# A mixture-of-experts kernel: row gathers moved behind the puts, three blocks ahead, and the sums' base copied by ScalarE

## The reference

```
x = layernorm(x + attention(x))      # q, k softmax; ctx = k^T v; y = q ctx Wo + bo
x = layernorm(x + moe(x))

logits = x @ wr.T                    # 8 experts
vals, idx = top_k(logits, 2)         # two experts for each row
gating = softmax over the two
cap = 5120                           # rows that an expert takes at most
xg = rows of x by expert
h = gelu(xg @ w1[e] + b1[e])         # 256 -> 1024
y = h @ w2[e] + b2[e]                # 1024 -> 256
out[row] += gating * y               # segment_sum over rows
```

## Time and profile before

| | |
|---|---|
| median of 3 runs | 2240.74 us (2238.51 to 2243.51) |
| profiled execution | 2238.88 us |
| its span | 2237.1 us |
| TensorE busy | 2024.5 us, 90% |
| VectorE busy | 1523.5 us, 68% |
| ScalarE busy | 1129.9 us, 51% |
| GpSimd busy | 1248.0 us, 56% |
| mean granted clock of TensorE | 0.973 |
| chain that ended last, by engine | PE 38%, issue 14%, POOL 8%, DVE 7%, DMA 3% |

### The profile page before, as it was taken

The page is one execution under the profiler, slowest core; times in us unless marked ns, Lnnn a source line. Parts: engine busy times, 40 slices in busy tenths (PEclk is TensorE's granted clock), DMA queues, the critical chain, the costliest instruction groups (busy, mean ns, idle before and its releaser), DMA issues.

```text
span 2237.1 us, 53012 instructions
## 1 busy us (share of the span) xinstructions
PE 2024.5 (90%) x15708; PEld 1938.2 (87%) x15709; DVE 1523.5 (68%) x4485; ACT 1129.9 (51%) x2519; POOL 1248.0 (56%) x1323
## 2 busy tenths in 40 slices
PE   7999899998678998999998999999999999999996
PEld 6888888887668988998898999989989989998996
DVE  3776777777546677668667666776777676666675
ACT  3566566565443444545454455454545445454553
POOL 1366666666645555555555555555555555555554
PEclk9999999999778999999999999999999999999998
DMA  5243334332124434334433443354354444443443
GB/s 178 84 145 124 106 123 146 107 123 86 58 70 154 144 103 142 115 111 125 132 108 106 147 121 116 112 154 124 116 157 124 126 119 128 128 134 117 138 129 99
DMA packets 306950, 272.74 MB, mean 122 GB/s; under 512 B 167331, under 2 KB 276094, under 8 KB 305744
## 3 DMA queue, kind: packets, MB, share of 16 engines
q1 hardware_dynamic: 253264, 171.59, 25.8%
q0 software_dynamic: 45200, 84.85, 12.2%
q10 hardware_dynamic: 8432, 15.73, 2.1%
HBM read 186.58 MB, written 102.26 MB: 129 GB/s over the span
## 4 chain that ended last, share of the span: by engine, by line
PE 38%; issue 14%; POOL 8%; DVE 7%; DMA 3%; another core or an unknown queue 2%; ACT 2%; DVEq 1%; SPq 0%; POOLq 0%; ACTq 0%
PE y_ps L1768 22%; PE h_ps L1752 15%; POOL rows L1442 5%; DVE h_lo L1683 2%; POOL rstd_b L1448 2%; POOL out L1466 1%; DMA stage<-rows 1%; DVE y L1649 1%; DMA x<-stage 0%; DVE rstd_b L1642 0%; DVE rstd_b L1640 0%; DMA base<-stage 0%; DVE put_idx L1647 0%; DMA rows<-x_rows,pick_idx 0%
## 5 line engine op out<-in xcount | busy, mean ns | idle before, releaser
L1556 ACT ACTIVATE h_ps<-h_ps,b_sb 128x256 f32<-128x256 f32 x1000 | 404.8, 445 | 620.4 <-PE h_ps L1752 607.5
L1768 PE MATMUL y_ps<-w_hi,h_hi 128*128 128x256 f32 x2000 | 576.2, 288 | 103.3 <-DVE h_lo L1683 77.0
L1752 PE MATMUL h_ps<-bt_hi,w_hi 128*128 128x256 f32 x2000 | 557.3, 279 | 5.4 <-issue 3.3
L1768 PE MATMUL y_ps<-w_hi,h_lo 128*128 128x256 f32 x2000 | 560.7, 280 | 0.3 <-issue 0.3
L1768 PE MATMUL y_ps<-w_lo,h_hi 128*128 128x256 f32 x2000 | 560.5, 280 | 0.0
L1752 PE MATMUL h_ps<-bt_hi,w_lo 128*128 128x256 f32 x2000 | 555.8, 278 | 1.2 <-issue 1.2
L1752 PE MATMUL h_ps<-bt_lo,w_hi 128*128 128x256 f32 x2000 | 555.8, 278 | 0.0
L1768 PEld LDWEIGHTS y_ps<-w_hi,h_hi 128*128 128x128 f32 x2000 | 380.0, 190 | 130.7 <-DVE h_lo L1683 93.7
L1442 POOL DMA_INDIRECT rows<-x_rows,pick_idx x250 | 247.6, 990 | 367.8 <-issue 328.0
L1752 PEld LDWEIGHTS h_ps<-bt_hi,w_hi 128*128 128x128 f32 x2000 | 377.4, 189 | 8.3 <-issue 5.7
L1768 PEld LDWEIGHTS y_ps<-w_lo,h_hi 128*128 128x128 f32 x2000 | 379.9, 190 | 0.0
(11 more groups left out here) (281 smaller groups left out, 3453.2 us busy)
## 6 DMA issues: line engine op xcount, KB each, us to landing
stage<-rows SPq DMA_DIRECT2D x126, 256.0 KB, 2.2
x<-stage SPq DMA_DIRECT2D x504, 64.0 KB
base<-stage SPq DMA_DIRECT2D x125, 256.0 KB
xt_raw<-in_x_t SPq DMA_DIRECT2D x32, 512.0 KB
x_raw<-in_x SPq DMA_DIRECT2D x64, 256.0 KB
x_rows<-x_sb SPq DMA_DIRECT2D x32, 512.0 KB
out<-alone SPq DMA_DIRECT2D x32, 512.0 KB
w_raw<-in_w ACTq DMA_DIRECT2D x14, 1024.0 KB
```

The source lines that it names most:

```text
L1556: nc.scalar.activation(half, half, ACT.Gelu_apprx_tanh, bias=b1_sb[:, bass.ds(e * FT + 2 * g + i, 1)]).then_inc(gelu_done, 1)
L1752: ins = nc.tensor.matmul(h_ps[:, g, (f % 2) * BLK:(f % 2 + 1) * BLK], w[:, c:c + P], v[:, k, :], start=(i == 0), stop=(i == 3 * DK - 1))
L1768: ins = nc.tensor.matmul(y_ps[:, t, :], v[:, g, h:h + P], w[:, c:c + D], start=(f == 0 and t == 0 and part == 0), stop=(f == FT - 1 and t ...
```

## The change

GpSimd issues the gather for block n+3 at the end of its block n, behind the puts (in an expert's first block behind the puts too, and before the wait for their landing). The gather of the third block is issued once ahead of the loop. To have the indices, VectorE copies pick_idx for it between bt_lo and the gates, not at its block's head. The slot table gets one more block of padding. SyncE reads the next block's rows from staging into a new buffer x1_next a block early, and ScalarE copies them to base after the add, behind its first h_hi (in an expert's second block behind its third, since the add is later there). To say that by block, ScalarE's first two blocks of an expert are written out ahead of its loop. Two small unused tensors change size and place.

```diff
@@ sync
-                def load_base(n):
-
-                    sp.wait_ge(sum_step, STEPS * n + 1)
-                    sp.dma_start(base[:, :, :], block_of(n).rearrange("(t p) d -> p t d", p=P)).then_inc(base_done, 16)
+                def load_next(n):
+                    sp.dma_start(x1_next[:, :, :], block_of(n).rearrange("(t p) d -> p t d", p=P)).then_inc(next_loaded, 16)
...
+                load_next(0)
                 with sp.Fori(0, total) as n:
-                    load_base(n)
-                    sp.wait_ge(gathered, 16 * BT * (n + 2))
+                    wait_apart(sp, base_done, n + 1)
+                    load_next(n + 1)
+                    wait_apart(sp, gathered, 16 * BT * (n + 2))
                     store_rows(n + 2, rows, stored)
                     wait_apart(sp, xt_ready, n + 1)
                     load_x4(n + 2)
@@ gpsimd
                 def gather(n):
                     pool.wait_ge(stored, 16 * (n - 1))
-                    wait_apart(pool, pick_ready, n - 1)
+                    wait_apart(pool, pick_ready, n - 2)
...
                 def take_up_sums(n):
-                    pool.wait_ge(base_done, 16 * (n + 1))
+                    pool.wait_ge(base_done, n + 1)
...
                 def first_body(n, lays=()):
-                    gather(n + 2)
                     root(n)
                     put(n)
+                    gather(n + 3)
                     for e in lays:
                         lay_table(e)
                     pool.wait_ge(put_done, 16 * BT * (n + 1) + 16)
                     take_up_sums(n)
                 def body(n, lays=(None, None)):
-                    gather(n + 2)
                     root(n)
                     take_up_sums(n)
                     if lays[0] is not None:
                         lay_table(lays[0])
                     put(n, 1)
+                    gather(n + 3)
@@ scalar
+                def lay_base(n):
+                    act.wait_ge(sum_step, STEPS * n + 1)
+                    act.wait_ge(next_loaded, 16 * (n + 1))
+                    nc.scalar.activation(base[:, :, :], x1_next[:, :, :], ACT.Copy).then_inc(base_done, 1)
-                def body(n, e, eu, load=False):
+                def body(n, e, eu, late_base=0, load=False):
                     for g in range(UNITS):
...
+                        if g == late_base:
+                            lay_base(n)
...
-                    with act.Fori(0, 4) as block:
+                    body(before, e, eu)
+                    body(before + 1, e, eu, 2)
+                    with act.Fori(2, 4) as block:
                         body(before + block, e, eu)
@@ vector, body
-                    pick(n + 2)
...
                             split_lo(n + 1)
-                            if e == 0 and turn == 3:
-                                dve.wait_ge(table_padded, 4 + E - 1)
+                            if e == 0 and turn in (2, 3):
+                                dve.wait_ge(table_padded, 4 + (1 if turn == 2 else E - 1))
+                            pick(n + 3)
                             gates(n + 1)
```

More of the change, by code:

```diff
@@ L30, in build @@
     CLOSED = NB - 3
-    TCOLS = MINI * BT + E * CAP // P + 2 * BT
+    TCOLS = MINI * BT + E * CAP // P + 3 * BT
     SLOTS = TCOLS * P
@@ L87, in build @@
         mini_table = keep("mini_table", [P, MINI * BT, EW], I)
-        table_in = keep("table_in", [P, E * EC + 2 * BT, EW], I)
+        table_in = keep("table_in", [P, E * EC + 3 * BT, EW], I)
+        keep("aside", [P, 24])
         rows = keep("rows", [P, BT, D])
@@ L1329, in build @@
             TCOLS = E * EC
-            table = sb("table", [P, BT + TCOLS + 2 * BT, EW], I)
+            table = sb("table", [P, BT + TCOLS + 3 * BT, EW], I)
             pick_idx, base_idx, put_idx = (sb(f"{n}_idx", [P, BT], I) for n in ("pick", "base", "put"))
@@ L1336, in build @@
             rstd, mean, minus_half = sb("rstd_b", [P, BT]), sb("mean_b", [P, BT]), sb("minus_half_b", [P, BT])
-            sb("spare", [P, 32])
+            sb("spare", [P, 24])
             xt_hi, xt_lo = sb("bt_hi", [P, DK, BLK], R), sb("bt_lo", [P, DK, BLK], R)
@@ L1345, in build @@
             x4 = sb("x4", [P, BLK // 32, D // 4])
+            x1_next = sb("x1_next", [P, BT, D])
             h_ps = ps("h_ps", [P, UNITS, 2 * BLK])
@@ L1355, in build @@
             x4_loaded, first_turned = sem("x4_loaded"), sem("first_turned")
+            next_loaded = sem("next_loaded")
             base_done, base_loaded = sem("base_done"), sem("base_loaded")
@@ L1396, in load_x4 @@
                 def load_x4(n):
-                    sp.wait_ge(stored, 16 * n)
+                    wait_apart(sp, stored, 16 * n)
                     by_band = block_of(n).rearrange("(g j) (c e) -> c j g e", j=32, c=4)
@@ L1422, in _ @@
                     load_x4(n + 2)
-                sp.wait_ge(x4_loaded, 64 * (total + 1))
+                wait_apart(sp, x4_loaded, 64 * (total + 1))
+                wait_apart(sp, next_loaded, 16 * (total + 1))
                 wait_apart(sp, put_done, 16 * BT * (total + 1) + 16)
@@ L1494, in _ @@
                 pool.wait_ge(first_stored, 16)
+                wait_apart(pool, stored, 16)
+                wait_apart(pool, first_turned, 1)
+                for t in range(BT):
+                    pool.indirect_dma_start(
+                        out=rows[:, t, :], out_offset=None, in_=x1_dram,
+                        in_offset=bass.IndirectOffsetOnAxis(ap=table_in[:, 2 * BT + t, 0:1], axis=0)).then_inc(gathered, 16)
                 def first_body(n, lays=()):
-                    gather(n + 2)
                     root(n)
                     put(n)
+                    gather(n + 3)
                     for e in lays:
@@ L1537, in _ @@
                 put(total)
-                pool.wait_ge(gathered, 16 * BT * (total + 1))
+                pool.wait_ge(gathered, 16 * BT * (total + 2))
             @program.scalar
@@ L1569, in expert @@
                     blocks, before = blocks_of(act, e)
-                    with act.Fori(0, 4) as block:
+                    body(before, e, eu)
+                    body(before + 1, e, eu, 2)
+                    with act.Fori(2, 4) as block:
                         body(before + block, e, eu)
-                    body(before + 4, e, eu, load)
+                    body(before + 4, e, eu, 0, load)
                     with act.Fori(5, blocks) as block:
@@ L1594, in pick @@
                 def pick(n):
-                    dve.wait_ge(gathered, 16 * BT * (n - 1))
+                    wait_apart(dve, gathered, 16 * BT * (n - 1))
                     V.tensor_copy(pick_idx[:, :], column(n + 1, 0)).then_inc(pick_ready, 1)
```

3 lines of the change are left out of this document (1 added, 2 removed).

## The result

| | median of the runs, us | runs |
|---|---|---|
| before | 2239.62 (2233.19 to 2243.51) | 4 |
| after | 2330.59 (2323.49 to 2350.87) | 4 |

The ratio is 1.042, 95% interval 1.035 to 1.049: slower, where 2165 us and faster was forecast. The kernel before does not always take this long: in one of the five sets of runs that follow it took 2122 us, in the other four 2226 to 2238 us, so a kernel is compared only with the kernel before of its own set.

A forecast was written before the change was run, and what follows sets the result against it. TensorE was taken as the bound, losing time waiting before `down(1)` for VectorE's h_lo behind a late root. Terms -88 + 8 + 0 + 4 = -76 us took 2238.88 to 2163, median 2165; own range 2142 to 2195, overall 2142 to 2230.

The forecast's parts named there:

- R3: Rival, chance 0.09: indirect DMAs over every block's head release VectorE and ScalarE 1.9 us late; 2366 us.
- Root earlier in each block: GpSimd's root starts 0.80 us earlier, closing TensorE's gap before `down(1)` in 113 blocks: 88 us saved, 54 to 98.
- What is late next: After the gap closes, TensorE's own pace sets the block: steady blocks 11.1 to 11.2 us apart.
- over 11.5 was the sign of being wrong: Sign that the forecast is wrong: TensorE's period from block to block stays over 11.5 us.
- Some 1.7 us of slack: GpSimd's block: its six indirect DMAs end at 2101.7, 1.7 us before the next variance at 2103.4.
- ScalarE's copy waits for nothing: ScalarE's 624 ns base copy behind the first h_hi finds the add done; cost taken as 0.
- ScalarE's code: Longer written-out ScalarE code may bring one more long wait at each of three jumps: 4 us taken, 0 to 13.
- Second blocks of an expert: There VectorE's add waits for base sums that come later: 1.0 us, 8 times, 8 us given back; 0 to 15.
- R1: Rival, chance 0.15: another step of VectorE's chain holds the second h_lo, 0.4 us left in each of 113 blocks; 2210 us.
- R2: Rival, chance 0.09: the moved gathers on GpSimd hold VectorE's add, taking 0.6 of the 0.9 us; 2219 us.
- R4: Rival, chance 0.07: GpSimd's gathers stay late behind pick_idx or the store, root as late as before; 2241 to 2253 us.

The follow-up runs named there:

- set A: First of the five sets of follow-up runs, all its kernels on one chip; the kernel before took 2122.35 us.
- sp_rows: Changed kernel without GpSimd's row gathers, SyncE reading rows in order instead: 2034.51 us, ratio 0.959; rerun 2108.45 us, 0.943.
- gather_only: Changed kernel with only the moved gathers and late pick_idx copy, base read by SyncE as before: 2080.37 us, 0.981; rerun 2459.82 us, 1.103.
- base_only: Changed kernel with gathers and pick_idx copy where they were before, base still copied by ScalarE from the early read: 2129.83 us, ratio 1.003.
- gate_swap: Changed kernel with gathers at GpSimd's block head behind y_raw, VectorE's root wait behind the second pair's h_lo: 2165.06 us, 0.970; rerun 2163.69 us, 0.968.
- set C: Third set of follow-up runs, varying how many and which DMAs GpSimd issues; the kernel before took 2236.14 us.
- set E: Last set of follow-up runs, on the same chip as set A; kernel before 2237.78 us, changed kernel again 2331.97 us, ratio 1.043.

## Why the prediction was wrong

The step that failed is the argument against R3, "the put at 1454.70 stands over a block's head too, and the add followed its data", which left it 0.09. That put does not stand over a head. The head is at 1453.01, and its y_raw started at 1453.32, 1.4 us before the put: the signal was through. The next one was not. The head, y_raw and ScalarE's first gelu of that block, in the trace of before:

```profile
1453.01 0.28 PE L1752 MATMUL h_ps<-bt_hi,w_hi 128*128 128x256 f32 x1
...
1453.32 0.69 DVE L1708 TENSOR_TENSOR y_raw<-y_ps,b_sb 128x512 f32<-128x512 f32 x1
...
1456.64 0.81 ACT L1556 ACTIVATE h_ps<-h_ps,b_sb 128x256 f32<-128x256 f32 x2 [6.57 <-PE h_ps L1752]
```

The gelu stands 3.63 us after the head, where 1.7 is usual, and 0.95 us after the put's end at 1455.69. The very block that was read against the rival shows it, as the earlier trace rows do (885.70 is 0.93 us after the put's end). Counting would have told: in 19 of 124 blocks of that trace an indirect DMA is in progress at the head, and in 12 of them y_raw starts over 1 us or the gelu over 2.2 us after it; of the other 105 it is 4. The count also shows what stays unexplained: in four of the 19 it is a gather of sums (base), and y_raw was prompt in all four, 1453.01 among them.

So the shift did not bring its 88 us, and the loss stands elsewhere than R3 had it. R3's formula, 1.9 us late less 0.9 us earlier in each of 113 blocks, puts the loss before `down(1)`. That gap did not change; the 100.8 us of the loop stand before `down(0)` and in TensorE's own stops, which neither the forecast nor R3 had. That R3's 2366 us comes near 2331 is in part luck.

Term by term:

- Root earlier in each block, 88 us: right in mechanism. The root is prompt, and in set A, where nothing is held, sp_rows gained 87.8 us. That the two agree so well is luck: sp_rows leaves out the gathers altogether, and gather_only, which has them, gained 42.0 us.
- What is late next: y_raw. It is 1.83 us later in the steady block, of which the prompt root gives 0.57 back (0.9 was forecast). The median distance of two heads rose from 12.00 to 13.18 us; 11.1 to 11.2 was forecast, and over 11.5 was the sign of being wrong.
- "Some 1.7 us of slack" on GpSimd was right in kind: its last gather ends before the next variance. It was beside the point: the question was where its DMAs lie, not whether they are done.
- ScalarE's copy waits for nothing: wrong here, 38.8 us in 86 blocks, because y_raw and the gelu start together, and 9.1 us once in the first block. In set A copy, longer code and early read cost 7.5 us together, against 0 + 4.
- ScalarE's code, 4 us: the waits with no known releaser, from which this was priced, did not come with the longer code: base_only has it and not one such wait.
- Second blocks of an expert, 8 us: waits of the adds for gathered sums rose from 10.5 to 16.5 us.
- R1, R2, R4 did not come: the second h_lo waits for y_raw's chain, the add follows y_raw by 0.12 us in the block shown, the gathers are not late. The 52 adds that ran beside an indirect DMA took 486 ns on average, the others 482.

## What to carry to other kernels

Ask of a moved indirect DMA not only whether it fits into GpSimd's block, but which signals of TensorE fall into its run; put such a run where nobody waits for one, and gate it behind the consumer if need be (gate_swap: 0.970). An outlier of before that the change turns into the rule is to be counted over all blocks, on every engine that waits there, before it is waved away. A kernel with these DMAs near its critical signals must be timed in more than one set of runs: gather_only is 0.981 in one and 1.103 in another.

## What the runs showed of the hardware

- In four of five sets (and in the first comparison) VectorE and ScalarE went on behind TensorE's signals mostly 0.8 to 1.3 us after the last of a run of GpSimd's indirect DMAs (1.0 us each, 0.3 apart), and TensorE itself stopped for some tenths of a us up to 1.3 us: 53.7 us more inside its first three `up` groups in the changed kernel. GpSimd's arithmetic (2.1 us), its plain DMAs (1.2 us for two) and SyncE's DMAs did not do this. That it is the signals which are held, and not the engines that wait, is inferred from these starts; no trace shows what holds them.
- Not every indirect DMA over a head does it: in the first trace of the kernel before, four gathers of sums over a head left y_raw prompt.
- In set A it did not occur, with the same kernels and the same DMA durations; the same chip showed it in set E. What differs between the sets was not found.
- Ahead of the loop, where 256 indirect DMAs write the slot table, it seems to be the same. That part took 604 us in sp_rows in set A and 664 us in the same kernel in set C, most of the 74 us between them. In set A none of its idle times has the releaser "remote"; in every other trace 38 to 47 of them do, 106 to 143 us. No run took these DMAs away.
- TensorE's granted clock was near full in all of them (0.97 to 0.99 on average), and 1.00 in the stretch of either kernel in which it lost most.
